# Moving sixteen multiplies of a graph layer's softmax from POOL to DVE

## The reference

```python
aff = einsum('bnhd,bmhd->bnhm', qh, kh) / sqrt(dh)        # 256 nodes, 16 heads, 20 neighbours
aff = where(mask, aff, NEG) + label_bias                  # per node and neighbour
w = softmax(aff, axis=-1)                                 # over the 20 neighbours
out_t = einsum('bnhm,bmf->bnhf', w, kv)
out = einsum('bnhf,hgf->bnhg', out_t, Wout) + bout
```

## Time and profile before

| what | value |
|---|---|
| median of 3 runs | 502.93 us (501.56 to 503.46) |
| the profiled execution's own time | 503.15 us |
| its span, first to last instruction | 501.4 us |
| PE busy | 412.6 us (82% of the span) |
| DVE busy | 309.7 us (62%) |
| ACT busy | 281.8 us (56%) |
| POOL busy | 175.4 us (35%) |
| mean granted clock of PE | 0.969 |

### The profile page before, as it was taken

One profiled execution on the slowest core, in us unless ns is written; L12 is line 12 of the kernel. 1 busy time (PEld: TensorE's weight loads), 2 busy tenths in 40 slices (PEclk: granted clock), 3 DMA queues, 4 the chain that ended last, 5 costly groups with the idle time before them and its releaser, 6 DMA issues. The chain is left out here.

```text
span 501.4 us, 9353 instructions
## 1 busy us (share of the span) xinstructions
PE 412.6 (82%) x3196; PEld 262.0 (52%) x3196; DVE 309.7 (62%) x846; ACT 281.8 (56%) x597; POOL 175.4 (35%) x226
## 2 busy tenths in 40 slices
PE   2777787988989999879996979778788889798974
PEld 2534454555646556445564546344455666576643
DVE  2464686864555646655376675776888777665721
ACT  2243254446545565445755586365767666668674
POOL 2812121331155331593369330641334322321200
PEclk9999899999999999999998899797999999899998
DMA  8920033000000000120002112001322313210000
GB/s 251 248 20 1 2 37 41 8 1 1 0 1 2 0 1 1 56 61 13 0 23 66 41 57 70 3 1 31 95 68 88 99 29 100 77 64 12 3 12 10
DMA packets 34527, 21.25 MB, mean 42 GB/s; under 512 B 22832, under 2 KB 31408, under 8 KB 34096
## 3 DMA queue, kind: packets, MB, share of 16 engines
q1 hardware_dynamic: 34480, 20.65, 15.8%
HBM read 16.97 MB, written 3.67 MB: 41 GB/s over the span
## 5 line engine op out<-in xcount | busy, mean ns | idle before, releaser
L965 ACT ACTIVATE pt<-psum 128x512 f32<-128x512 f32 (+1 forms) x192 | 106.1, 558 | 94.0 <-PE psum L1507 46.1
L1135 DVE TENSOR_REDUCE negm<-psum 128x2 f32<-128x512 f32 x128 | 84.5, 683 | 38.3 <-PE psum L1437 23.4
L760 POOL TENSOR_TENSOR pairsum<-pt 128x256 f32<-128x256 f32 x64 | 46.7, 730 | 141.1 <-ACT pt L965 137.7
L771 POOL COPY big<-mT 32x1024 bf16<-32x1024 bf16 x32 | 33.1, 1035 | 118.7 <-ACT mT L957 118.3
L1483 PE MATMUL psum<-big 128*128 128x256 bf16 (+1 forms) x256 | 50.3, 266 | 4.6 <-POOL big L771 3.4
L1132 DVE TENSOR_REDUCE negm<-psum 128x3 f32<-128x384 f32 x64 | 34.8, 554 | 16.8 <-PE psum L1443 16.1
L1502 PE MATMUL psum<-big 64*128 64x256 f32 x256 | 39.1, 396 | 2.4 <-ACT pt L965 2.2
L1176 DVE TENSOR_TENSOR oT<-psum,rden 128x256 f32<-128x256 f32 x64 | 26.5, 414 | 17.5 <-ACT rden L981 16.9
L1406 PE MATMUL psum<-hT,pt 128*128 128x256 f32 x128 | 34.8, 409 | 2.1 <-DVE negm L1135 1.2
L1531 PE MATMUL psum<-pt,room 128*64 128x256 f32 x256 | 36.5, 408 | 0.0
L1111 DVE COPY big<-psum 128x512 f32<-128x512 f32 x32 | 22.0, 689 | 20.3 <-PE psum L1406 20.1
(11 more groups left out here) (184 smaller groups left out, 859.8 us busy)
## 6 DMA issues: line engine op xcount, KB each, us to landing
big<-scratch SPq DMA_DIRECT2D x96, 96.0 KB
scratch<-room SPq DMA_DIRECT2D x48, 64.0 KB, 2.0
adj_s<-adj SPq DMA_DIRECT2D x16, 110.0 KB, 3.9
w0s<-w SPq DMA_DIRECT2D x1, 1536.0 KB, 9.6
w3s<-w SPq DMA_DIRECT2D x1, 1088.0 KB, 12.0
room<-wqk SPq DMA_DIRECT2D x2, 512.0 KB, 6.5
xT<-x_t SPq DMA_DIRECT2D x4, 128.0 KB, 6.5
w1s<-w SPq DMA_DIRECT2D x1, 512.0 KB, 9.9
```

The costliest lines, as they stand in the source:

```text
L760: nc.gpsimd.tensor_tensor(pairsum[:, u % SUM_RING, :], pt[:, pt_slot(u), 0:T], pt[:, pt_slot(u), T:2 * T], ALU.add).then_inc(pairsum_ready, 1)
L771: nc.gpsimd.tensor_copy(stacks[SHIFT_ROW:128, b % ROOMS, 0, GH * g:GH * (g + 1), :], mT[SHIFT_ROW:128, at % 2, :].unsqueeze(1).broadcast_t ...
L965: nc.scalar.activation(pt[:, pt_slot(u), 0:width], psum[:, ST_BANK + u % 2, 0:width], ACT.Exp, scale=EXP_SCALE[layer]).then_inc(pt_ready, 1)
L1135: ins = nc.vector.tensor_reduce(negm[:, g, 0:NT, j], bk.rearrange("p (q k) -> p q k", q=NT), AX_X, ALU.max, negate=True)
```

## The change

The sixteen multiplies of step 3 leave POOL's part of `layer1` and stand in DVE's part, at the same ticks, behind the sum and the reciprocal of the same tick. DVE waits for its own reciprocal, for the transposes of unit `w - 2`, and, before the very first multiply, for the clear of `wgt` at the start (`more_consts`). POOL's own list of signals that it has to wait for before some later steps (`latest`) no longer holds `wgt_ready`.

```diff
@@ POOL, layer1 @@
-                        if tick in L1_WEIGHTS:
-
-                            w = L1_WEIGHTS.index(tick)
-                            pool.wait_ge(arec_ready, first + w + 1)
-                            if w >= 2:
-                                wait_full(pool, ("wT", w - 2, b))
-                            nc.gpsimd.tensor_tensor(wgt[:, w % 2, :, 0:NG], aff[:, w],
-                                                    arec[:, w, :].unsqueeze(2).broadcast_to([128, H, NG]),
-                                                    ALU.mult).then_inc(wgt_ready, 1)
-                            latest[wgt_ready] = first + w + 1
                         yield
@@ DVE, layer1 @@
                             nc.vector.reciprocal(arec[:, w, :], asum[:, w, :]).then_inc(arec_ready, 1)
+                        if tick in L1_WEIGHTS:
+
+                            w = L1_WEIGHTS.index(tick)
+                            dve.wait_ge(arec_ready, first + w + 1)
+                            if w >= 2:
+                                wait_full(dve, ("wT", w - 2, b))
+                            elif first + w == 0:
+                                dve.wait_ge(more_consts, 1)
+                            nc.vector.tensor_tensor(wgt[:, w % 2, :, 0:NG], aff[:, w],
+                                                    arec[:, w, :].unsqueeze(2).broadcast_to([128, H, NG]),
+                                                    ALU.mult).then_inc(wgt_ready, 1)
                         if tick == L1_TICKS - 1:
```

## The result

The changed kernel takes 505.22 us (median of 18 runs, 501.82 to 511.05) against 502.88 us (18 runs, 499.77 to 507.28) in the same rounds. The ratio is 1.0047 with a 95% interval of 1.0025 to 1.0068, or 1.3 to 3.4 us longer. The forecast was 503.2 us, 0.3 us longer, in a range of 499.3 to 506.3: the time lies in the range, the sum was some 2 us short. An interval that reaches 0.68% does not show "within half a per cent". Four of the 18 runs, 510 us and longer, are over 1.5% above the kernel's fastest and are not counted in the ratio.

The account below looks back on a forecast made before the run. PE's order of work sets the time, with DVE level or behind. Batches 0 to 3 sum to 1.4 - 0.9 - 1.1 + 0.9 = +0.3 us: 503.45 profiled, 503.2 as median, range 499.3 to 506.3.

Parts of the forecast that it names:

- The multiply costs the queue: DVE's queue in units 0 and 1: each multiply delays the next instruction 0.52 us, or 0.91 when it waits for POOL.
- Unit 2 of batch 1: Batch 1: PE's 1.90 us wait for this multiply, behind POOL's four copies, goes whole; the batch sums to -0.9 us.
- the first multiply of batch 2: Batch 2: PE starts at 266.11 instead of 267.95; of its 4.04 us wait about 2 us should remain.
- The eight multiplies of units 2 and 3: DVE's queue behind the maxima PE needs next: costed at nothing; without this cover 3.3 us.
- Batch 0: +1.4: Batch 0: two multiplies make the maxima for L1466 1.4 us later, and PE, already waiting there, loses 1.4 us.
- the stretch of L1162: Batch 1: POOL's multiply no longer stretches this DVE instruction, -0.4 us, leaving PE +1.0 at the maxima.
- The half clock: PE at 1.2 of 2.4 GHz after idling in batch 2: a stretch coming or going moves the time up to 1.7 us.
- Batches 2 and 3: Batch 2 gains 1.1 us through an earlier L1135; batch 3 loses 0.9 us at L1135, for which PE's L1437 waits.
- The wait for `wgt`: PE at L1701: waits for its multiply no longer exceed 0.5 us in batches 0, 1 and 3.
- DVE's share is hidden: Faster rival: the maxima have more slack, so PE keeps 4.6 us directly; 496.6 to 498.3 us, chance 0.24.
- DVE and POOL hold each other up: Slower rival: multiplies and POOL's L812 and L819 delay each other, +5.7 us, 508.6; decides from 505.4; chance 0.20.
- theory C: Account tested in the follow-ups: the change does nothing and the time difference is an accident of the clock.

Follow-up runs that it names:

- second measurement: The changed kernel run again with nothing altered, against the kernel before: 506.74 us, ratio 1.0088.
- the spare multiplies: Kernel before, POOL's multiplies kept, with DVE also making those of units 0 and 1 into an unread tile: ratio 1.0093 to before.
- the split by batches: Two kernels against before, all four multiplies on DVE only in batches 1 and 2 (0.9973) or only in batches 0 and 3 (1.0044).

## Why the prediction was near, and where it was short

**Held.** The multiply costs the queue 0.91 us beside POOL, and 0.53 alone (0.52 forecast). Unit 2 of batch 1 was priced at -1.9 and is -2.07 where it was moved alone, and the first multiply of batch 2 brought its wait down to 2.21 ("about 2"). The wait in batch 3 is 1.63 ("over 1.5"), those at the maxima in batches 0 and 1 are 1.79 and 1.99 ("over 1"). The eight multiplies of units 2 and 3 cost nothing that shows: with them alone batch 0's stretch is the same to 0.01 us, and the kernel is faster, not slower. (The working's 152.0 and 215.1 are the ends of unit 0's transposes alone, not of units 0 and 1; nothing in the sum hangs on it.) The Trainium skill's page Perfetto Trace Analysis ("Optimizing Scalar/DVE Operations") doubts that moving work between these two engines helps; the runs agree for units 0 and 1 (1.0061) and not for units 2 and 3 (0.9938).

**Batch 0: +1.4, measured +1.90 in the wait.** PE starts on the transposed maxima 1.90 us later, counted from the stretch's start, in both profiles. The delay of 1.43 was right, but it pushed the cast L1150 under POOL's L760, 0.36 us more, which the working left out; 0.1 is spread over smaller rows. In batch 1 the same cast met POOL's clears (0.53), so the 0.4 that I had taken off for the stretch of L1162 came back there: +1.49 at the maxima instead of +1.0. After unit 2's wait is gone this leaves -0.78, near the forecast of -0.9, where the clock stays up.

**The half clock: placed in no term.** This is the step that failed. I priced such a stretch at up to 1.7 us and let it move the range either way; I looked for it in batch 2, where it might go. It came behind the waits that the sum itself had made longer, in batch 0 or in batch 1, 1.4 to 1.6 us. The terms with it in are +3.28 and -0.78 in one profile, +1.91 and +0.85 in the other, against +1.4 and -0.9. The two together are +2.5 and +2.76 against +0.5: in the two profiles that is the missing 2 us, 0.6 of it by the waits (+1.90 and -0.78 where the clock stays up) and 1.4 to 1.6 by the clock. That the timed runs lost their time in these parts is not shown. The mean granted clock of the runs counted in the first ratio is 0.9653, against 0.9655 in before's runs of the later rounds: no more half clock over the launch, only perhaps in other places. In the second measurement it is 0.9613 against 0.9666, and with units 0 and 1 alone 0.959 against 0.967: there more half clock is on record. So the clock's part in the medians stays open. Where units 0 and 1 of batch 0 or 1 stayed on POOL and DVE got nothing else ahead of the maxima, no trace shows a half clock in that batch. It is absent also in three traces that have the long waits (units 0 and 1 alone, the spare multiplies, batch 1 of the split by batches), and what decides is open.

**Batches 2 and 3** were forecast at -1.1 and +0.9 (the terms given for batch 2 add up to 271.18 rather than 271.1, which makes -1.0) and came out at -1.43 and +1.62, then +0.22 and -0.12. The waits moved as said; the stretches wander with the clock, and I do not take them as shown one by one.

**The wait for `wgt`** in batch 1 was to fall below 0.5 us and is 1.01: the first multiply there took 0.87 beside POOL. It cost nothing by itself, since the maxima are later still. Counted from the start of the span, batch 0's layer ends 1.20 us late ("1.4") and batch 2's 1.01 us early ("0.6"), but 2.08 us of that were gained ahead of the graph layer by code that didn't change: without them it is +3.28 and +1.06, and the test should have been put from the start of the stretch.

**The rivals.** "DVE's share is hidden" falls: it is true of units 2 and 3 and false of units 0 and 1. "DVE and POOL hold each other up" was right that POOL is held too and wrong in the size: the longest L812 and L819 take 1119 and 1048 ns, against 866 and 731 before, but on average 877 and 746 instead of 860 and 727, not 1 us. The times, 505.22 and 506.74 us, lie about and over the 505.4 from which I had let it decide; the stretches of the two profiles put that down to the wait for the maxima and the clock behind it. That the difference is an accident (theory C) falls by the two halves of the change, whose intervals lie on either side of 1.

## What to carry to other kernels

When work is moved to another engine, price each of its places in that engine's queue by what stands behind it and who reads that; a mean busy share of 62% hid that half of the moves cost and the other half won. Move only the instructions whose waits the profile shows: one multiply of sixteen had most of the gain. And where a move makes a wait of TensorE longer in a stretch that so far ran at full clock, put a price on a half-clock stretch right there.

## What was not expected of the hardware

A tiny instruction can be held like a large one, which the forecast had read the earlier trace rows but not carried to its own terms: the cast of 128x16 numbers, 0.17 us, took 0.53 beside POOL's L760 and again beside its clears of `big`. And POOL is held in turn: L760 took 1.03 us behind a multiply on DVE. A multiply that met POOL's row of four copies was held by one of them, not by all four: 1.26 us with units 2 and 3 on DVE, 1.00 in the changed kernel, where the four took 4.30 us in batch 1 instead of 3.99. And two waits of TensorE of equal length, to 0.01 us, with the same instructions ahead, were followed in one execution by full clock and in the other by 1.2 GHz.
